# State products and router logits as column tiles, with feature-major input, in a two-layer retention and expert kernel

## Time and profile before

| | us |
|---|---|
| median of 3 runs | 1480.71 |
| lowest, highest | 1479.6, 1485.88 |
| profiled execution | 1474.93 |
| its span, first to last instruction | 1473.1 |
| TensorE busy in the span | 1197.4 (81%) |
| VectorE, ScalarE, GpSimd busy | 910.4, 716.5, 736.8 |

### The profile page before, as it was taken

One profiled execution on the slowest core, in us unless ns is written; L12 is line 12 of the kernel. 1 busy time (PEld: TensorE's weight loads), 2 busy tenths in 40 slices (PEclk: granted clock), 3 DMA queues, 4 the chain that ended last, 5 costly groups with the idle time before them and its releaser, 6 DMA issues. The chain is left out here.

```text
span 1473.1 us, 33745 instructions
## 1 busy us (share of the span) xinstructions
PE 1197.4 (81%) x10118; PEld 1079.8 (73%) x10119; DVE 910.4 (62%) x2572; ACT 716.5 (49%) x1859; POOL 736.8 (50%) x913
## 2 busy tenths in 40 slices
PE   7989898998319887883799999996199999999940
PEld 6988888887318887883477666675099999999940
DVE  4777676766345555553578888864576666666626
ACT  2343333423225555552466666643166666666627
POOL 0265656555634565555016666657524444444446
PEclk9998888888558999997899999986599999999975
DMA  8121111100032222221333211101221111111138
GB/s 239 37 61 44 32 32 36 52 28 19 29 98 77 79 82 74 77 76 68 101 95 105 65 56 47 68 25 41 69 56 53 56 52 56 52 56 52 48 101 265
DMA packets 81530, 101.72 MB, mean 69 GB/s; under 512 B 15154, under 2 KB 59698, under 8 KB 81010
## 3 DMA queue, kind: packets, MB, share of 16 engines
q1 hardware_dynamic: 55730, 60.96, 14.4%
q0 software_dynamic: 17280, 35.69, 7.4%
q10 hardware_dynamic: 8448, 4.20, 1.0%
HBM read 60.93 MB, written 44.11 MB: 71 GB/s over the span
## 5 line engine op out<-in xcount | busy, mean ns | idle before, releaser
L1081 POOL DMA_INDIRECT expert_out<-e_ysb,e_idx x284 | 295.8, 1042 | 329.7 <-ACT e_ysb L1120 180.6
L1229 PE MATMUL banks<-e_x_hi,e_w_hi 128*128 128x256 f32 x852 | 256.5, 301 | 2.2 <-DVE e_h L1200 1.6
L1229 PE MATMUL banks<-e_x_hi,e_w_lo 128*128 128x256 f32 x852 | 243.4, 286 | 5.8 <-issue 5.8
L1229 PE MATMUL banks<-e_x_lo,e_w_hi 128*128 128x256 f32 x852 | 243.4, 286 | 3.1 <-issue 3.0
L1239 PE MATMUL banks<-w_dn,e_h 128*128 x1704 | 222.2, 281 | 22.2 <-ACT e_ysb L1125 16.1
L1200 DVE TENSOR_TENSOR e_h<-banks,e_sgl 128x512 f32<-128x512 f32 x213 | 146.4, 688 | 148.2 <-ACT e_sgl L1107 77.6
L1239 PEld LDWEIGHTS banks<-w_dn,e_h 128*128 128x128 f32 x1704 | 208.5, 196 | 28.8 <-issue 28.6
L1107 ACT ACTIVATE e_sgl<-banks 128x512 f32<-128x512 f32 x213 | 127.9, 600 | 158.6 <-PE banks L1229 114.6
L1229 PEld LDWEIGHTS banks<-e_x_hi,e_w_lo 128*128 128x128 f32 x852 | 165.3, 194 | 6.2 <-issue 6.2
L1229 PEld LDWEIGHTS banks<-e_x_hi,e_w_hi 128*128 128x128 f32 x852 | 166.3, 195 | 3.8 <-issue 3.2
L1229 PEld LDWEIGHTS banks<-e_x_lo,e_w_hi 128*128 128x128 f32 x852 | 166.4, 195 | 2.5 <-issue 2.4
(11 more groups left out here) (278 smaller groups left out, 2591.6 us busy)
## 6 DMA issues: line engine op xcount, KB each, us to landing
e_xg<-scattered SPq DMA_DIRECT2D x142, 130.0 KB, 2.0
b_cy<-expert_out SPq DMA_DIRECT2D x32, 256.0 KB
f_y<-expert_out SPq DMA_DIRECT2D x32, 256.0 KB, 4.3
expert_out<-e_ysb,e_idx POOLq DMA_INDIRECT x284
a_xb<-in_x SPq DMA_DIRECT2D x16, 256.0 KB, 2.9
out<-f_x ACTq DMA_DIRECT2D x16, 256.0 KB, 4.2
scattered<-in_spare SPq DMA_DIRECT2D x2, 1040.0 KB
scattered<-in_spare SPq DMA_DIRECT2D x16, 130.0 KB
```

The costliest lines, as they stand in the source:

```text
L1081: nc.gpsimd.indirect_dma_start(out=expert_out, out_offset=bass.IndirectOffsetOnAxis(ap=idx[d.slot][:, i:i + 1], axis=0), in_=ysb[d.slot][: ...
L1229: mm = nc.tensor.matmul(banks[bank_of(j, c)][:, i * ROWS:(i + 1) * ROWS], w_[c.slot][:, g, f:f + P], x_[c.slot][:], start=(k == 0), stop=( ...
```

## The change

- **State products.** In `retention0` one product of 128 by 256 becomes four, one for a head, each with 32 columns of `kt` as weights and the head's 64 columns of `v` as moving operand; they write partitions 32h to 32h+31 of the same 64 columns of `U`. VectorE spreads these 64 columns over the four blocks while it multiplies by `m_blk`. In `retention1` each of the six products becomes four of 32 by 32.
- **Logits.** `w_r`, padded with zeros to 32 columns, becomes the weights and `router.xT` moves: four products of 32 by 128, one for a chunk, in the four column tiles. ScalarE copies the 128 by 128 result to `lgT`, and TensorE transposes it once; `choose` reads its 8 columns from every 32. `router.lg_mm` is now raised by that transpose.
- **Feature-major input.** `retention0` loads x also as `x_T` (features by tokens, laid out outside the device), so its four transposes a step and their waits are gone; `x_hi` and `x_lo` are made from SBUF.
- The identity's load moves behind the first load of x and of the weights.

```diff
@@ retention0, ScalarE
+                    def turned_logits(d):
+                        act.wait_ge(lgT_mm, d.n + 1)
+                        wait_count(act, router.lg_mm, d.n)
+                        nc.scalar.copy(lgT[:], T1[:, 0:P]).then_inc(lgT_there, 1)
...
-                            act.wait_ge(xT_mm, z.n + 1)
-                            nc.scalar.copy(x_hi[z.odd][:], T1).then_inc(x_hi_there, 1)
+                            act.wait_ge(s_x[z.odd], z.half * 16 + 16)
+                            wait_count(act, g_mm, z.n - 1)
+                            nc.scalar.copy(x_hi[z.odd][:], xT[z.odd][:]).then_inc(x_hi_there, 1)
...
+                        if d and a:
+                            turned_logits(d)
@@ retention0, VectorE
-                        nc.vector.tensor_tensor(S[c % 2][:], U[:, 0:H0 * DV0], m_blk[:], ALU.mult).then_inc(S_there, 1)
+                        nc.vector.tensor_tensor(S[c % 2][:].rearrange("p (h n) -> p h n", h=H0),
+                                                U[:, 0:DV0].unsqueeze(1).to_broadcast([P, H0, DV0]),
+                                                m_blk[:].rearrange("p (h n) -> p h n", h=H0), ALU.mult).then_inc(S_there, 1)
@@ retention0, TensorE
-                        nc.tensor.matmul(U[:, 0:H0 * DV0], kt[:, c, :], v[b.odd][:, c, :],
-                                         start=(c == 0), stop=(c == CH - 2), skip_group_check=True).then_inc(U_mm, 1)
+                        for h in range(H0):
+                            rows = slice(DK0 * h, DK0 * (h + 1))
+                            mm = nc.tensor.matmul(U[rows, 0:DV0], kt[:, c, rows], v[b.odd][:, c, h * DV0:(h + 1) * DV0],
+                                                  start=(c == 0), stop=(c == CH - 2), skip_group_check=True)
+                        mm.then_inc(U_mm, 1)
...
-                            for j in range(CH):
-                                mm = nc.tensor.transpose(T1[:, j * P:(j + 1) * P], xb[z.odd][:, j, :], c_ident[:])
-                            mm.then_inc(xT_mm, 1)
...
+                            for i in range(CH):
+                                mm = nc.tensor.matmul(T1[32 * i:32 * i + 32, 0:P], w_r[:], router.xT[:, i * P:(i + 1) * P],
+                                                      start=True, stop=True, skip_group_check=True)
+                            mm.then_inc(lgT_mm, 1)
                         if b:
                             outputs(b, 2)
                         if d:
+                            pe.wait_ge(lgT_there, d.n + 1)
+                            wait_count(pe, router.idx_there, d.n)
                             if b:
                                 pe.wait_ge(S_there, (CH - 1) * b.n + CH - 1)
-                            router.logits_mm(pe, LG, d)
+                            nc.tensor.transpose(LGT, lgT[:], c_ident[:]).then_inc(router.lg_mm, 1)
@@ retention1, TensorE
-                                mm = nc.tensor.matmul(U[:, j * P:(j + 1) * P].rearrange("p (g k d) -> p g k d", k=2, d=DH1),
-                                                      kt[:, i, :], vz[b.odd][:, i, :, 0:3:2, :],
-                                                      start=(i == 0 and j == 0), stop=(i == j), skip_group_check=True)
+                                for g in range(4):
+                                    rows = slice(32 * g, 32 * g + 32)
+                                    mm = nc.tensor.matmul(US[rows, j, :].rearrange("p (k d) -> p k d", d=DH1),
+                                                          kt[:, i, rows], vz[b.odd][:, i, g, 0:3:2, :],
+                                                          start=(i == 0 and j == 0), stop=(i == j), skip_group_check=True)
```

More of the change, by code:

```diff
@@ L340, in logits_mm, with choose @@
                 last.then_inc(self.lg_mm, 1)
-            def choose(self, dve, bank, t):
+            def choose(self, dve, lg, t):
                 ch = self.chain
@@ L551, in retention0 @@
                 m_blk = sb("m_blk", [P, H0 * DV0])
-                w_r = sb("wr", [P, E])
-                xb = [sb(f"xb{i}", [P, CH, D]) for i in range(2)]
+                w_r = sb("wr", [P, P // CH])
+                lgT = sb("lgT", [P, P])
+                xT = [sb(f"xT{i}", [P, T]) for i in range(2)]
                 x_hi = [sb(f"x_hi{i}", [P, T], F32R) for i in range(2)]
@@ L622, in body @@
                             sp.dma_start(w_raw[:], w_proj).then_inc(s_wp, 16)
+                            sp.dma_start(c_ident[:], ident).then_inc(s_id, 16)
                             for to, src in small:
-                                sp.dma_start(to[:], src).then_inc(s_w, 16)
+                                sp.dma_start(to[:] if to is not w_r else to[:, 0:E], src).then_inc(s_w, 16)
                             for to, src in consts:
@@ L709, in body @@
                             nc.scalar.copy(router.xT[:], T0).then_inc(router.xT_there, 1)
+                            if not a:
+                                turned_logits(d)
                             act.wait_ge(x1_there, d.n + 1)
@@ L814, in body @@
                             dve.wait_ge(x_hi_there, z.n + 1)
-                            nc.vector.tensor_tensor(x_lo[z.odd][:], T1, x_hi[z.odd][:].bitcast(F32), ALU.subtract
-                                                    ).then_inc(xT_ev, 1)
+                            nc.vector.tensor_tensor(x_lo[z.odd][:], xT[z.odd][:], x_hi[z.odd][:].bitcast(F32), ALU.subtract
+                                                    ).then_inc(x_there, 1)
                             if isinstance(z.n, int) and z.n == 0:
@@ L982, in body @@
                             project_tokens(B[2:4], a, 1).then_inc(g_mm, 1)
+                        if d:
+                            pe.wait_ge(router.xT_there, d.n + 1)
+                            if isinstance(d.n, int) and d.n == 0:
+                                pe.wait_ge(s_pad, 1)
+                            for i in range(CH):
+                                mm = nc.tensor.matmul(T1[32 * i:32 * i + 32, 0:P], w_r[:], router.xT[:, i * P:(i + 1) * P],
+                                                      start=True, stop=True, skip_group_check=True)
+                            mm.then_inc(lgT_mm, 1)
                         if b:
@@ L1350, in retention1 @@
                 B = psum[4:8]
-                LG, RK = U[:, 384:384 + CH * E], U[:, 416:416 + CH * E + E]
+                US = U[:, 0:(CH - 1) * 32].rearrange("p (c n) -> p c n", c=CH - 1)
+                LGT, LGX, RK = U[:, 128:256], U[:, 256:384], U[:, 416:416 + CH * E + E]
+                LG = LGX.rearrange("p (c w) -> p c w", c=CH)[:, :, 0:E]
+                lgT = sb("lgT", [P, P])
+                lgT_mm, lgT_there = sem("lgT_mm"), sem("lgT_there")
                 VB = O[:, 0:CH * H1]
@@ L1392, in _ @@
                         nc.gpsimd.memset(vz[i][:], 0.0).then_inc(zero_there, 1)
+                    pool.wait_ge(s_early, n_w)
+                    nc.gpsimd.memset(w_r[:, E:], 0.0).then_inc(zero_there, 1)
                     norm.set_up(pool)
@@ L1446, in _, with turned_logits @@
                     act.wait_ge(zero_there, 2)
+                    def turned_logits(d):
+                        act.wait_ge(lgT_mm, d.n + 1)
+                        wait_count(act, router.lg_mm, d.n)
+                        nc.scalar.copy(lgT[:], LGT).then_inc(lgT_there, 1)
                     def body(ts):
@@ L1454, in body @@
                             nc.scalar.copy(router.xT[:], T0[:, :]).then_inc(router.xT_there, 1)
+                            if not b:
+                                turned_logits(d)
                         if a:
@@ L1462, in body @@
                             router.copy_rows(act, d, x3_there)
+                            if b:
+                                turned_logits(d)
                         if b:
@@ L1592, in _ @@
                     pe.wait_ge(set_there, 2)
+                    pe.wait_ge(zero_there, 3)
                     def scores(b, h):
@@ L1692, in body @@
                                 pe.wait_ge(S_there, b.n + 1)
-                            router.logits_mm(pe, LG, d)
+                            wait_count(pe, router.idx_there, d.n)
+                            for i in range(CH):
+                                mm = nc.tensor.matmul(LGT[32 * i:32 * i + 32, :], w_r[:], router.xT[:, i * P:(i + 1) * P],
+                                                      start=True, stop=True, skip_group_check=True)
+                            mm.then_inc(lgT_mm, 1)
                         if c2 and (a or b):
@@ L1699, in body @@
                             project_out(c2)
+                        if d:
+                            pe.wait_ge(lgT_there, d.n + 1)
+                            nc.tensor.transpose(LGX, lgT[:], c_ident[:]).then_inc(router.lg_mm, 1)
                         if b:
@@ L1917 @@
     arrays = {
-        "x": g["L0_attn_x"],
+        "x": g["L0_attn_x"], "x_T": g["L0_attn_x"].transpose(0, 2, 1),
```

53 lines of the change are left out of this document (23 added, 30 removed).

## The result

The changed kernel takes **1526.8 us** (median of 4, 1525.7 to 1537.9) and the kernel before, on the same chip, 1480.2 (1475.6 to 1485.9). The ratio is **1.035, 95% interval 1.031 to 1.038**: slower, by about 47 us. The forecast was 1471.8 with a range of 1457 to 1487. The profiled execution has a span of 1525.0 us, 51.9 more than before.

What follows compares the result with a forecast made beforehand. The prediction took TensorE as busiest in both retentions, with 11 first-retention steps paced by GpSimd's scatters. Savings of 3.5, 2.75, 1.6 and 1.0 us, 8.9 off the 1480.71 median, gave 1471.8 us, range 1457 to 1487.

Steps and rivals of the forecast that it cites:

- The transposes of x: First retention: four transposes a step go, 0.36 us each step, counted in full in five steps before the scatters, 1.8 us.
- State products: First retention: each product takes 0.34 us as column tiles instead of 0.43, so 0.27 us off a step of three.
- Logits of the first retention: First retention: 0.54 us with column tiles and transpose instead of 0.87, so 0.33 off; ScalarE's copy costs nothing or 0.1 to 0.2.
- Paced steps: First retention, 11 steps whose scores stall until GpSimd's scatter batch ends: 0.25 us saved in each, 2.75 us in all.
- My quarter of 0.96: Share of TensorE's 0.96 us saving a step assumed to reach the end in the 11 paced steps, taken as 0.25 us.
- absorbed: Rival, chance 0.17: paced steps give nothing, the copy costs 0.1 to 0.2 a step, ends give half; 3 us off, 1478.
- Ends of the retentions: Last steps of each retention, with no other work left: shorter logits save 0.4 us in four places, 1.6 us.
- Second retention: Logits save 0.33 us a step, which arrives only in the steps before the scatters begin: 1.0 us faster in all.
- the rival: Slower case, chance 0.21: in the second retention late logits delay GpSimd's second pair and TensorE's results; 1486 to 1491 us.
- the hold: Second retention: TensorE's results held until 1.7 us behind GpSimd's last scatter; the slower rival decides if this covers 864 us.
- States of the second retention: Second retention: 48 small records take 1.3 us instead of 1.44, between bounds of 0.9 and 1.7.
- full reach: Rival, chance 0.22: first retention's stall moves with TensorE or its low clock shortens; 10.5 us instead of 2.75, 1464 to 1450.

Runs made afterwards that it cites:

- e11: Kernel before with the feature-major x alone, so four transposes of x less in each step of the first retention; ratio 0.997 to the kernel before.
- e16: Kernel before with the new first retention and one GpSimd scatter pair there moved behind the next scores, on a chip with paced steps; ratio 0.964.
- e18: Kernel before with only one GpSimd scatter pair of the first retention moved behind the next scores, on a chip with paced steps; ratio 0.969.
- e10: Kernel before with the new first retention and one GpSimd pair there moved behind the next scores, on a chip without paced steps; ratio 0.997.
- e9: Kernel before with only one GpSimd pair of the first retention moved behind the next scores, on a chip without paced steps; ratio 1.002.
- e12: The changed kernel itself on the other kind of chip, where the kernel before takes about 1350 us; ratio 1.033 to the kernel before.
- e4: Changed kernel with GpSimd's second pair of the second retention waiting for the logits' column tiles instead of their transpose; ratio 1.004 to the kernel before.
- e8: Kernel before with only one GpSimd pair of the first retention moved behind the next scores, on a chip without paced steps; ratio 1.001.

## Why the prediction was wrong

*The transposes of x (0.36 a step, 1.8 us in all).* This failed at "nothing but TensorE's work lies between scores and scores, so it all counts". VectorE sets the middle of such a step (e11). Measured: nothing.

*State products (0.34 for 0.43).* The block was 0.25, at the low end of my 0.24 to 0.38; but I charged the way in once and no way out, and both ends cost 0.1 in the neighbours. By the end of the projections a step is 0.15 us ahead (L881 came 13.78 us after the scores, L988 comes 13.63 after), where I had 0.27.

*Logits of the first retention.* Right, 0.33 forecast: they take 0.48 for 0.87 with a copy of 0.26 and no wait behind it, and L898 behind them pays 0.1 for the way out, so 0.3 in a step (81.67 to 83.80 before, 80.36 to 82.20 now). So 0.47 a step and not 0.96; by the last scores before 86 us 1.6 us and not 3.5.

*Paced steps (2.75).* The reading was right that GpSimd's batch ends the stall (1.97 us behind the sixth scatter; e16 and e18 break it by taking two scatters out). My quarter of 0.96 was too much: the 11 steps gave nothing, and by the last scores (345.64 for 345.11) the 1.6 us were gone as well and 0.5 more. This is the rival "absorbed".

*Ends of the retentions (1.6).* Nothing came: from the last scores to the first product of `experts(0)` 89.3 us for 87.9, and from the last states to that of `experts(1)` 87.5 for 80.9. On the chips of 1350 us the first of these is 80.4 in e10 and 80.6 in e9.

*Second retention (1.0 us faster; measured 39 us slower in its 15 steps).* The failed step is "the logits save 0.33 again, but ahead of L1708": the late logits were given no price there, though the rival named what waits for them. In that rival I followed the late logits to the pair and the pair to TensorE's held results: the right place, at 0.9 to 1.4 us a step. The wait that decided was another, ScalarE's L291 for the last scatter out of the row buffer. It closes a ring of logits, four pairs, row buffer, normed rows, transposes, logits, which took 19.1 us in every other step before, as long as the step itself. The 2.4 us of lateness first used up the 1.1 us that GpSimd had waited in it and then made it 1.3 longer; with the low clock that came along, the 11 steps with scatters lost 3.5 us each. The row that showed it, ScalarE's idle time before L291 released by "DMA scattered", was in the trace of before in about every other step; I had read ScalarE only in the first retention. The "point from which it decides" that I gave (the hold) was wrong, since e12 loses the same with no hold. In the steps ahead of the scatters the saving did come, 0.46 us in one (17.07 for 17.53).

*States of the second retention (1.3 us).* The 48 records take 0.63 us in e4's row, so less than both my bounds (0.9 and 1.7). By the Trainium skill (TensorEngine Tiling (Array Packing), Instruction Overhead), 60 cycles a matmul make 1.2 us of them, an estimate from that page; this trace does not agree with it for records in four tiles beside each other. In the ring it gave nothing in the changed kernel, since L330 waits for ScalarE then.

The direction of the forecast was wrong for a reason that I had weighed at 0.21, and at an eighth to a fourth of its price: 1486 to 1491 against 1526.8. One figure of the rival "full reach" was also off in itself: 1464 less 11 times 1.6 is 1446, not 1450.

## What to carry to other kernels

Before an operation is moved, list every engine that waits for it, pacing waits included, and follow each until it comes back to the operation: if it does, the steps can't on average be shorter than the sum of that ring, and once the waits inside it are used up, a microsecond in it is a microsecond of every step. A wait that only paces an engine should hang on the earliest event that does its work; here one semaphore was worth 3%. A saving on the busiest engine counts only between the points where another engine hands over, so look for that engine's unbroken runs first.

## What the runs showed of the hardware

**Chips differ by 8% on one program.** On two chips the kernel before took 1350 us, on the others 1468 to 1480, with the same durations of single instructions (GpSimd's power 3.41, a scatter 0.96 to 1.04). On the 1350 chips I saw no result of TensorE stay back behind GpSimd's scatters: in e12 none in the retentions was over 0.4 us late, and the scores run through with the six scatters in place,

```profile
190.76 1.17 PE L879 MATMUL banks<-a_qr,a_kT 32*128 32x128 f32 x32
...
208.56 1.17 PE L879 MATMUL banks<-a_qr,a_kT 32*128 32x128 f32 x32
```

at 17.8 us a step against 24.0. The paced steps are only half of the difference. The last scores come 60 us sooner (285.5 in e8, whose moved pair changes nothing on such a chip, and 345.1 before), and another 53 us go between the first product of `experts(0)` and the states (225.5 in e8, 278.8 before), where GpSimd also issues indirect DMAs one after another; I did not follow those. What in the chip does it no run here shows.

**The low clock multiplies a wait.** In e12 a stand of 2.8 us was followed by 10 us at half clock, and the step was 7 us longer, more than twice the stand. **Column tiles** of 32 moving columns run at 13 ns a record at full clock (48 in 0.63 us, e4), and a group costs its neighbours some 0.1 us on either side (L863 and L898 above).
